# Router logits carried as extra columns of two projections, the choice made on raw logits, and odd chunks' outputs two pairs further on

## What is computed

```python
# attention: chunked retention, 8 heads of 16 channels, chunks of 64 tokens
q, k, v = h @ Wq, h @ Wk, h @ Wv                     # h = layernorm(x)
attn = einsum(qc, kc) * D                            # within a chunk
o = einsum(attn, vc) + einsum(qc * decay_q, S)       # plus the state before it
S = decay_s * S + einsum(kc * decay_k, vc)
x = x + o @ Wo
# experts: E = 8, hidden 256, the two best of eight
logits = layernorm(x) @ Wg; probs = softmax(logits)
top_w, top_i = top_k(probs, 2); top_w = top_w / (sum(top_w) + 1e-8)
y = sum_e combine[t, e] * (relu(h_t @ W1[e]) ** 2) @ W2[e]
x = x + y
```

## Time and profile before

| | |
|---|---|
| median of 3 runs | 290.26 us (289.76 to 290.81) |
| the profiled execution, its own time | 288.95 us |
| its span | 287.2 us |
| busy PE / DVE / ACT / POOL | 274.8 / 222.4 / 179.3 / 206.1 us |
| granted TensorE clock, mean | 0.998 |

### The profile page before, as it was taken

How to read it: one execution, slowest core, us unless ns; L and a number is a source line. 1 busy time by engine, 2 the same in 40 slices (tenths; PEclk the granted TensorE clock), 3 DMA queues, 4 the chain that set the end, 5 groups by cost and what they waited for, 6 DMA issues and landing times.

```text
span 287.2 us, 8936 instructions
## 1 busy us (share of the span) xinstructions
PE 274.8 (96%) x3662; PEld 216.4 (75%) x3662; DVE 222.4 (77%) x569; ACT 179.3 (62%) x257; POOL 206.1 (72%) x165
## 2 busy tenths in 40 slices
PE   7999868899999999999999999999999999999995
PEld 5685547678887788777887788777887788878883
DVE  2759758995769875996869965896859768998783
ACT  2345476565782688555974677556875567586861
POOL 2115889879959697769968699569968668566452
PEclk9999999999999999999999999999999999999999
DMA  7329062222250261204440240103420252043101
GB/s 227 120 82 295 5 214 71 86 63 96 70 147 2 78 185 60 89 11 126 128 147 2 79 179 23 59 5 103 157 75 2 77 152 92 19 130 130 75 0 73
DMA packets 13577, 26.80 MB, mean 93 GB/s; under 512 B 1120, under 2 KB 6624, under 8 KB 13536
## 3 DMA queue, kind: packets, MB, share of 16 engines
q1 hardware_dynamic: 13536, 26.23, 28.5%
HBM read 24.00 MB, written 2.23 MB: 91 GB/s over the span
## 4 chain that ended last, share of the span: by engine, by line
PE 52%; POOL 21%; issue 16%; DVE 5%; DMA 2%; ACT 2%; POOLq 1%; DVEq 0%; ACTq 0%
POOL act_lo L1062 17%; PE h_ps L333 7%; PE y_ps L348 6%; PE h_ps L335 6%; PE h_ps L334 5%; PE y_ps L354 5%; PE y_ps L349 5%; PE bank L480 2%; PE bank L492 2%; PE bank L413 2%; POOL x_lo L1032 2%; POOL rstd L1016 1%; PE bank L445 1%; DMA scale<-scratch 1%; PE y_ps L312 1%
## 5 line engine op out<-in xcount | busy, mean ns | idle before, releaser
L1062 POOL TENSOR_TENSOR act_lo<-act_f,act_hi 128x512 fp32r<-128x512 f32 x112 | 145.9, 1325 | 47.7 <-ACT act_f L950 47.6
L760 DVE SCALAR_TENSOR_TENSOR act_s<-h_ps,scale 128x1024 f32<-128x1024 f32 x64 | 77.9, 1217 | 31.1 <-issue 13.6
L945 ACT ACTIVATE act_hi<-act_s 128x1024 fp32r<-128x1024 f32 x64 | 67.9, 1061 | 33.7 <-DVE act_s L760 33.1
L950 ACT ACTIVATE act_f<-act_s 128x1024 f32<-128x1024 f32 x64 | 67.0, 1046 | 0.0
L333 PE MATMUL h_ps<-x_hi,w_lo 128*128 128x512 f32 x128 | 54.1, 422 | 1.0 <-DVE attn L653 1.0
L348 PE MATMUL y_ps<-act_hi,w_lo 128*128 128x512 f32 x128 | 53.9, 421 | 0.0
L335 PE MATMUL h_ps<-x_hi,w_hi 128*128 128x512 f32 x128 | 50.5, 395 | 0.0
L334 PE MATMUL h_ps<-x_lo,w_hi 128*128 128x512 f32 x128 | 50.5, 394 | 0.0
L349 PE MATMUL y_ps<-act_hi,w_hi 128*128 128x512 f32 x128 | 50.3, 393 | 0.0
L354 PE MATMUL y_ps<-act_lo,w_hi 128*128 128x512 f32 x128 | 40.2, 395 | 0.1
L1016 POOL TENSOR_TENSOR rstd<-variance,minus_half 128x4 f32<-128x4 f32 x16 | 17.9, 1119 | 19.1 <-DVE variance L617 18.9
(11 more groups left out here) (121 smaller groups left out, 402.3 us busy)
## 6 DMA issues: line engine op xcount, KB each, us to landing
scale<-scratch SPq DMA_DIRECT2D x32, 512.0 KB, 4.0
x_t_in<-x_tr SPq DMA_DIRECT2D x8, 256.0 KB, 4.8
x_all<-x SPq DMA_DIRECT2D x8, 256.0 KB, 4.6
out<-out_sb SPq DMA_DIRECT2D x8, 256.0 KB, 4.1
scale<-w SPq DMA_DIRECT2D x1, 768.0 KB, 4.8
cst<-constants SPq DMA_DIRECT2D x1, 417.0 KB, 6.0
cst<-constants SPq DMA_DIRECT2D x1, 256.0 KB, 2.8
scale<-w SPq DMA_DIRECT2D x1, 256.0 KB, 6.7
```

The lines of the kernel that those rows point to most:

```text
L760: nc.vector.scalar_tensor_tensor(out=act_s[:, u % 2], in0=h_ps[:, u % 2], scalar=0.0, in1=scale[:, f % 2, e].unsqueeze(1).to_broadcast([P, ...
L945: nc.scalar.activation(act_hi[:, u % 4], act_s[:, u % 2], ACT.Square).then_inc(act_hi_ready, 1)
L950: nc.scalar.activation(act_f[:, u % 2], act_s[:, u % 2], ACT.Square).then_inc(act_f_ready, 1)
L1062: nc.gpsimd.tensor_tensor(act_lo[:, u % 4, n], act_f[:, u % 2, n], act_hi[:, u % 4, n].bitcast(F32), ALU.subtract).then_inc(pool_low_ready, 1)
```

## The change

The router's logits are no longer a matmul of their own. They are a sum of two parts: x times the centred Wg, which comes as 8 extra columns of the V projection (`w_vg`), and the attention's output times Wo times the centred Wg, which comes as 8 extra columns of the output projection (`w_out` is 136 wide). `x_all` is 136 wide for each group; `add_attention` adds both parts, and the raw logits stand in its last 8 columns, before the division by the standard deviation. Four groups of 136 columns don't fit a PSUM bank, so the fourth lies in another one (`v_place`, `out_place`), and q and k are projected in two slots. The choice is made on raw logits (`rank_experts`, `mark_chosen`), the root of the denominator alone is taken on POOL (`root_denominators`), and the two weights are half-exponentials times it. Outputs of odd chunks go two pairs further on in the partitions, and `copy_o` brings them back in two half-height copies.

On PE, the places and the slots:

```diff
+        def v_place(s, g):
+            if g == GROUPS - 1:
+                return ((y_ps[:], h_bank[3])[s] if s < 2 else bank1[:])[:, 0:WIDE]
+            return ((bank1[:], h_bank[2])[s] if s < 2 else bank2[:])[:, WIDE * g:WIDE * (g + 1)]
+        def out_rows(pair, c):
+            at = (pair + 2 * c) % PAIRS
+            return slice(PW * at, PW * (at + 1))
...
-            def route(s):
...
-                    last = pe.matmul(route_bank(s)[:, EXPERTS * g:EXPERTS * (g + 1)], x_sum[:, s % SUM_RING, P * g:P * (g + 1)],
-                                     wg_whole[:], start=True, stop=True)
...
                     if n == 1:
-                        project_qk(a)
+                        project_k(a)
                     if n == 3:
-                        transpose_k(a)
+                        project_q(a)
                     if n == 4:
-                        project_v(a)
+                        transpose_k(a)
+                    if n == 5:
+                        project_v(a)
...
             center_piece(1)
-            route(0)
             state_updates(1)
             center_piece(2)
             center_piece(3)
+            center_piece(4)
+            transpose_roots(0)
             w1_product(0, 0)
-            center_piece(4)
             outputs_within(1, (0, 1))
-            transpose_roots(0)
```

From tile 2 on, `project_q(a)` waits for `x2_ready` (the last `add_attention`), `project_k(a)` for the scores before it, and `project_v(a)` as before for `q_m_ready` and `q_d_ready`, and for `x_hi_ready`. On DVE, the loop and two functions:

```diff
                     add_attention(p)
                     statistics(p, 1)
-                if a < TILES:
-                    decay_q(a)
                 scale_h(f, 1)
                 low(u)
+                if p < TILES:
+                    rank_experts(p)
+                    shift_logits(p)
                 if a < TILES:
                     decay_k(a)
+                    decay_q(a)
                 scale_h(f, 2)
                 low(u + 1)
                 if p < TILES:
-                    shift_logits(p)
+                    weigh(p)
+                    mark_chosen(p)
                 scale_h(f, 3)
                 low(u + 2)
                 if p < TILES:
-                    choose(p)
+                    spread_roots(p)
                 if a < TILES:
                     decay_scores(a, decay_order(a)[0:1])
                 scale_h(f, 4)
                 low(u + 3)
                 if a < TILES:
-                    decay_scores(a, decay_order(a)[1:2])
-                if p < TILES:
-                    spread_roots(p)
-                if a < TILES:
-                    decay_scores(a, decay_order(a)[2:])
+                    decay_scores(a, decay_order(a)[1:])
...
-                    last = nc.vector.tensor_scalar(logits[:, g], l_ps[:, g], top[:, g:g + 1],
+                    last = nc.vector.tensor_scalar(shifted[:, g], best[:, g], best[:, g, 0:1],
                                                    rstd[:, 1, s % STAT_RING, g:g + 1], ALU.subtract, ALU.mult)
...
             def spread_roots(s):
-                dve.wait_ge(root_ready, s + 1)
+                dve.wait_ge(r_denom_ready, s + 1)
+                dve.wait_ge(expd_ready, s + 1)
+                nc.vector.tensor_tensor(root[:], half_expd[:], r_denom[:].unsqueeze(2).to_broadcast([P, GROUPS, TOP]),
+                                        ALU.mult).then_inc(spread_step, 1)
```

`rank_experts` is four MAX8; `weigh` is a reduction and three operations on 128 x 4; `mark_chosen` is four searches for an index, a cast and a comparison. On ACT, `copy_v`, `exponentiate`, `copy_o`, the end of the part ahead of the loop, and the loop:

```diff
+                    nc.scalar.copy(x_all[:, s % X_RING, g, P:WIDE], v_place(s, g)[:, P:WIDE])
...
+                nc.scalar.activation(half_expd[:], shifted[:, :, 0:TOP], ACT.Exp, scale=0.5).then_inc(expd_ready, 1)
...
+                nc.scalar.copy(o_t[:, s % 2, :, 0], outs[0])
+                nc.scalar.copy(o_t[0:P // 2, s % 2, :, 1], outs[1][P // 2:])
+                nc.scalar.copy(o_t[P // 2:, s % 2, :, 1], outs[1][0:P // 2]).then_inc(o_t_ready, 1)
...
             copy_roots(0)
+            copy_o(1)
+            copy_k(2)
             high_second()
-            copy_o(1)
-            mask_q(2)
-            copy_k(2)
             high_qk()
...
                 square(u)
                 if f >= 1 and a < TILES:
-                    mask_q(a)
                     copy_k(a)
                 if p < TILES:
                     high_x(p)
+                if a < TILES:
+                    mask_q(a)
+                if p < TILES:
+                    exponentiate(p)
                 square(u + 1)
                 if a < TILES:
                     copy_v(a)
                 if f >= 1:
                     copy_y(f - 1)
                 square(u + 2)
-                if p < TILES:
-                    exponentiate(p)
                 square(u + 3)
```

On POOL:

```diff
             low_x(0)
+            root_denominators(0)
+            pool.wait_ge(combine_ready, 1)
             low_piece(1)
-            root_shares(0)
-            pool.wait_ge(combine_ready, 1)
...
                 low(u + 1)
                 low(u + 2)
                 if p < TILES:
-                    root_shares(p)
+                    root_denominators(p)
                 low(u + 3)
```

More of the change, by code:

```diff
@@ L412, in project_v @@
                 for g in range(GROUPS):
-                    last = pe.matmul(v_bank(s)[:, P * g:P * (g + 1)], x_t_in[:, s % XT_RING, P * g:P * (g + 1)],
-                                     w_center[:, 2], start=True, stop=True)
+                    last = pe.matmul(v_place(s, g), x_t_in[:, s % XT_RING, P * g:P * (g + 1)], w_vg, start=True, stop=True)
                 last.then_inc(v_done, 1)
@@ L491, in outputs_before @@
                             rows = slice(PW * pair, PW * (pair + 1))
-                            last = pe.matmul(chunk_bank(s, c)[rows, CHUNK * g:CHUNK * (g + 1)],
+                            last = pe.matmul(chunk_bank(s, c)[out_rows(pair, c), CHUNK * g:CHUNK * (g + 1)],
                                              state[rows, s % 2, :, 2 * g + c], chunk_of(q_d[rows, b], 2 * g + c),
@@ L538, in slot @@
                         transpose_x2(p)
-                    if n == 5:
-                        route(p)
                     if n == 12:
@@ L709, in choose, with weigh, weighed @@
+            def weigh(s):
+                def weighed(n):
+                    dve.wait_ge(weigh_step, WEIGH_STEPS * s + n)
                 dve.wait_ge(expd_ready, s + 1)
-                for g in range(GROUPS):
-                    last = nc.vector.max(best[:, g], expd[:, g])
-                last.then_inc(choose_step, 1)
-                nc.vector.tensor_reduce(total[:], expd[:], AX_X, ALU.add).then_inc(choose_step, 1)
-                chosen_step(1)
-                for g in range(GROUPS):
-                    last = nc.vector.max_index(best_at[:, g], best[:, g], expd[:, g])
@@ L803, in _ @@
             decay_scores(1, decay_order(1)[1:2])
-            choose(0)
+            weigh(0)
+            mark_chosen(0)
+            spread_roots(0)
             decay_scores(1, decay_order(1)[2:])
-            spread_roots(0)
             mask_updates(1)
```

269 lines of the change are left out of this document (140 added, 129 removed).

## The result

The changed kernel takes **335.92 us** (median of 4 runs, 333.8 to 338.19), the kernel before on the same chip 290.04 (289.76 to 290.81): 1.158 times as long, 95% interval 1.150 to 1.166. The forecast was 330, range 305 to 341. The profiled execution took 333.8 us; its span is 332.0, against 287.2.

What follows compares the result with a forecast made beforehand. PE, busy 96%, bounded the kernel; new waits on ACT, POOL and DVE would outweigh its saving: 288.95 + 11.4 + 19.5 + 1.1 = 320.9, plus 8 for the clock and 1.3 to the median, 330 us; range 305 to 341.

Steps and rivals of the forecast that it cites:

- Saved on PE: PE in each tile: no route, wider projections, shorter outputs_before; 1.15 us less if PE never waits.
- The 0.6 us of the tiling rule: outputs_before on PE: independent array positions would save the whole 0.6 us a tile; the forecast took 0.36.
- Steps 1 to 6: Tiles f = 1 to 5: loop over ACT, POOL and DVE delays w1_product(f, 5); 36.8 us a tile, 19.5 in all.
- 0.9 us lost at `w2_product`: PE wants w2_product(8f) at 12.95 but gets it at 13.85, behind copy_v and copy_y on ACT.
- The holds: Small DVE operations with SBUF operands last until the running POOL operation ends: 1.30 us against 0.23.
- The first tile: Late high_second on ACT delays low_second on POOL to 42.0; w1_product(0, 5) starts at 66.4, costing 11.4 us.
- The last two tiles: In f = 6 copy_y moves past the point where PE wants it, 1.1 us; f = 7 adds 0.
- The clock: PE's clock falls in most of seven gaps where PE stands still; 8 us, between 0 and 15.
- the term 1.5 to 2.5: Work lost on PE at each clock fall, if half the clock lasts 3 to 5 us: 1.5 to 2.5 us.
- the clock stays up: Rival: PE's clock does not fall through the gaps; 322 us, chance 0.22.
- the second rival's 307: Rival: DVE not held by POOL at shift_logits and the roots; 34.6 us a tile, 307 or 309, chance 0.18.
- The rival of the other side: PE never waits because the power comes early enough, and the saving stands; 282 us, chance 0.04.

Runs made afterwards that it cites:

- c4: Changed kernel, same work, engines' order altered, among it both powers earlier on POOL and low(u + 2) waiting for the finished roots; 283.30 us, ratio 0.978.
- e8: Kernel before with only the odd chunks' outputs two pairs further on in the partitions and copy_o in three copies; 288.01 us, ratio 0.996.
- e3: Changed kernel with copy_y in front of copy_v on ACT; 334.02 us, ratio 1.154 to the kernel before.
- e2: Changed kernel with POOL waiting for the finished roots before it starts low(u + 3); 313.77 us, ratio 1.084 to the kernel before.
- c2: Changed kernel, same work in another engine order, with x_lo behind low(u + 3) and mark_chosen behind scale_h(f, 3); 292.27 us, ratio 1.011 to the kernel before.
- e6: Changed kernel with twelve useless matmuls on PE before the wait of w1_product(f, 5) for the scores, in six tiles; 326.78 us, ratio 1.130.
- e5: Changed kernel with high_second in front of copy_o(1) and copy_k(2) on ACT; 330.14 us, ratio 1.140 to the kernel before.
- e4: Changed kernel with root_denominators in front of low(u + 2) on POOL; 307.17 us, ratio 1.060 to the kernel before.
- c1: Changed kernel, same work, order altered: both powers earlier, spread_roots behind the second scores, copy_y and high_second earlier, prologue reordered; 300.67 us, ratio 1.039.
- e1: Changed kernel with spread_roots put back behind the second group of decay_scores on DVE; 309.53 us, ratio 1.068 to the kernel before.
- e9: Changed kernel with decay_k and decay_q in front of shift_logits on DVE, and exponentiate behind square(u + 1) on ACT; 333.74 us, ratio 1.153.

## Why the prediction was right

The mechanism was right in its steps, and the time lies in the range; some sizes were off, and a part of the agreement is luck.

**Saved on PE: 1.15 us forecast, 1.0 measured.** c4's tile is 31.87 to 31.90 us, the forecast for a PE that never waits was 31.7. `outputs_before` gave 0.29 us, not 0.36 (158.52 - 157.66, and again in e8): the prediction subtracted the lengths of two blocks, and the time to the next matmul was 1.15, not 1.22; the eight instructions of `project_out` went from 0.81 to 0.84 us, those of `project_v` from 0.81 to 0.92 (134.89 - 133.97), together 0.14 for the 0.10 in the sum. The 0.6 us of the tiling rule of the Trainium skill (TensorEngine Tiling (Array Packing), Key Properties) does not show: twice as many positions made the block a quarter shorter, not half.

**Steps 1 to 6.** Against the tile at full clock, in t: `project_v` 11.0 (10.6 forecast), the start of `copy_y` 13.45 (13.25), `w2_product(8f)` 14.15 (13.85), end of `low(u + 2)` 18.6 (18.3), end of the power 19.6 (19.35), `w1_product(f, 5)` 23.16 (23.1), from there to the next tile 13.9 us (13.7). The tile is 37.06 for 36.8. Two sizes were off and nearly cancelled, which is luck. POOL's power for the variance begins at t = 6.85 (129.81), not 6.3: "`low` of the two units before, which don't move" was wrong, for they waited 0.32 us for ACT, whose `square` begins 0.6 us later behind the third copy of `copy_o`. With it `project_v` is 0.4 us late. And `copy_v` with its small copies takes 1.24 us, not 1.54. A third, `weigh`, is held twice (1.20 and 1.20 us), which the sum did not have and which costs nothing here, since DVE waits for POOL's power anyway. Its term "0.9 us lost at `w2_product`" is no loss either (e3); it was not added in the sum.

**The holds** were the step with the least behind it, two rows of the trace before. e2 shows them: 1.23 and 1.25 us become 0.17 and 0.22 when POOL stands still. The rule of the Trainium skill that the prediction names (SBUF — State Buffer, Who interferes with whom) also has a second half, that an instruction with at most one SBUF input, outside the two-port modes, is not held; the rows of c2 agree: beside a running POOL, `FIND_INDEX8` keeps its 0.16 us (its row names two tiles, but the trace has an instruction of its own in front of it, `MATCH_VALUE_LOAD`, that loads the values) and `attn`, with its other operand in PSUM, its 0.68. `shift_logits`, with one tensor in SBUF and two scalars for each partition, is held; no run shows which of the two is the reason.

**The first tile: 11.4 us forecast, 15.4 measured.** The step that was mis-sized is the start of `low_second`, 42.0 forecast, 44.33 measured. `project_out(1)` came at 39.77, not 37.5: the clock was at half level from 32.2 to 35.4 already, which the forecast did not have (3.2 us of work at half speed), `w1_product(0, 0)` came at 31.5, not 30.8, and `copy_o(1)` in three copies made PE wait 1.2 us (0.8 before). From there on the forecast's intervals hold (24.4 us from `low_second` to `w1_product(0, 5)`, 24.8 measured). A fall at 69.7, behind that wait, adds the rest: e6, without it, starts the second tile 1.5 us earlier. e5 shows what the place of `high_second` is worth: 4.9 us at `w1_product(0, 5)`, the largest part found, though not all.

**The last two tiles: 1.1 forecast, 1.8 measured.** PE's only wait over 0.25 us there is that for `copy_y` (1.78 us at 288.30).

**The clock: 8 us forecast, 8 to 9 measured** (e6: ratio 1.130 instead of 1.158). It fell behind four of the five standstills of 3.2 us, not behind that of f = 2. It stayed at 0.50 for 3.4 us (107.2 to 110.6 in f = 1, f = 4 and f = 5 alike) and in f = 3 for 6.8 us (182.3 to 189.1), and the tiles are 1.3 to 2.5 us longer for it (38.35 to 39.58 against 37.06), so the term 1.5 to 2.5 was right. The rival "the clock stays up", 322, is what e6 forces in the five tiles: 326.8 comes out, and the rest to 322 is mostly the first tile. Its argument, that a standstill of 2.2 us brought no fall, holds for one trace only: behind the 1.8 us of f = 6 the clock fell in e4, e5, e6 and c1, and did not in the changed kernel, e1, e2 and e3; behind 2.0 us in the first tile it fell in c4 and did not in the kernel before, c2 and e5.

**Three readings of the rows were off**, and none moves the sum. The last matmul of the earlier trace rows ends at 283.94, and 0.53 over 286.0 to 287.2 puts the fall at 286.1, so 2.1 us after PE stopped, not 2.4. The longest standstill of the kernel before is 2.0 us in its list of waits (at 41.40), not 2.2. And the second rival's 307 lacks the 1.3 us up to the median that the other sums have.

**The sum.** In the profiled runs 44.8 us were added, of which 40 had been forecast. Without the falls behind the waits for the scores the tiles f = 1 to 5 gave 20.9 (5 x 4.18) instead of 19.5, the first tile 13.9 instead of 11.4, the last two 1.8 instead of 1.1; these falls gave 8.2 instead of 8. So the term that was most mis-sized is the first tile, by 2.5 us; some 1 us of it is the clock again, which was still low behind the wait of 10.9 us (`project_v(2)` took 2.15 us instead of 1.17). The rest of the 5.9 us between 330 and 335.9 is mostly that the profiled execution was the fastest of the four, 2.1 us under the median where the forecast had 1.3; its mean clock was 0.949, that of the others 0.934 to 0.944.

**The rival of the other side** gave 282 if the power came early enough and the saving stood. That state exists: c4, at 283.3, with DVE not held at the roots and the power at t = 15.0, ahead of the 16.3 that the rival asks for in that case. It needed no faster operation, only other places.

What stays open: why the clock kept its level behind one standstill and fell behind the next of the same length. It is not a matter of the tile: in e3 the one without a fall is f = 3, and in e5 the clock fell in all five. Open is also what limits `outputs_before` at 0.86 us.

## What to carry to other kernels

When an engine's queue gets a new wait, follow the waited-for result back through every engine that makes it, and ask for each what stands in front of it in its own order; here one call in front of the first scores joined PE to POOL's and ACT's queues, and one line moved (e1 or e4) gave back more than half of a loss of 46 us. The length of a wait in the list is not its price: e3 took away 0.6 us a tile and gained 0.3; e9 shortened the wait of 10.9 us by 7.3 through another order and moved `w1_product(0, 5)` by 0.5 us; e5 shortened it by 5.1 through its cause, the late `low_second`, and gained 4.9. See whether what comes behind the wait starts earlier, too. And before judging a change by its time, look for the order that lets its saving show: the same work took 336 us and 283 us.

## What the runs showed of the hardware

- Small DVE operations that are held pay for each POOL instruction that they meet, one by one: the four `shift_logits` of 128 x 8 took 0.87 us beside an idle POOL (c4), 1.77 when the first met `x_lo`, and 3.33 (c1) and 3.83 us (e9) when POOL ran three instructions without a pause and three of the four were held. For them the number of operations counted more than their size.
- Not everything is held: `FIND_INDEX8` took 0.16 us beside a running POOL (c2, above), the conversion behind it 0.65 instead of 0.17, the comparison 1.26 instead of 0.23.
- In the kernel before the two copies of `copy_o` took 0.65 us together (the row below); now there are three, two of them from 64 partitions to 64 others; they start 0.39 and 0.38 us apart and last 0.36 to 0.37 each (e8): half the partitions cost as much as all.
- Twelve matmuls without use in each of six standstills made the kernel 9 us faster: the granted clock stayed at its upper level, 2.4 GHz, behind all six (e6).

```profile
100.68 0.65 ACT L916 COPY o_t<-bank 128x256 f32<-128x256 f32 x2 [2.76 <-PE bank L492]
```
